# A two-layer attention on sorted edges: PSUM operands, rank one-hots per pass, lifted scores, a running maximum in two parts

## What is computed

```
h = (x @ W).reshape(n_nodes, H, C)
s_src, s_dst = einsum(h, a_src), einsum(h, a_dst)
e = s_src[src] + s_dst[dst]
e = where(e > 0, e, 0.2 * e)
e_max = segment_max(e, dst)
e_exp = exp(e - e_max[dst])
denom = segment_sum(e_exp, dst)
out = segment_sum(e_exp / denom[dst] * h[src], dst) + bias
```

## Time and profile before

| | us |
|---|---|
| median of 3 runs | 9747.82 |
| lowest and highest | 9736.4, 9757.34 |
| profiled execution: span | 9753.4 |

### The profile page before, as it was taken

One profiled execution on the slowest core, in us unless ns is written; L12 is line 12 of the kernel. 1 busy time (PEld: TensorE's weight loads), 2 busy tenths in 40 slices (PEclk: granted clock), 3 DMA queues, 4 the chain that ended last, 5 costly groups with the idle time before them and its releaser, 6 DMA issues. The chain is left out here.

```text
span 9753.4 us, 157815 instructions
## 1 busy us (share of the span) xinstructions
PE 6819.7 (70%) x40294; PEld 4632.6 (47%) x40295; DVE 4925.6 (51%) x14201; ACT 1511.9 (16%) x2248; POOL 3772.6 (39%) x3460
## 2 busy tenths in 40 slices
PE   0466304666666549999977777767777769996999
PEld 0345203344332225555546666656666635553555
DVE  6877805555554432222227788878888830113011
ACT  1222101111111111000002222222222200000000
POOL 1777875555542200000007677747777600000000
PEclk6688756776776669999988888878888879997999
DMA  0222101222221315686751111111111146653666
GB/s 15 54 70 70 35 9 59 76 78 71 71 71 59 55 49 163 173 197 173 179 139 46 45 44 45 44 44 45 45 44 45 41 121 190 190 170 104 190 192 183
DMA packets 871576, 901.10 MB, mean 92 GB/s; under 512 B 421539, under 2 KB 820226, under 8 KB 864867
## 3 DMA queue, kind: packets, MB, share of 16 engines
q1 hardware_dynamic: 753541, 637.16, 23.8%
q0 software_dynamic: 109664, 179.92, 8.3%
q10 hardware_dynamic: 8064, 80.29, 2.0%
HBM read 722.84 MB, written 93.87 MB: 84 GB/s over the span
## 5 line engine op out<-in xcount | busy, mean ns | idle before, releaser
L1900 POOL DMA_INDIRECT d_row_ring<-table_att,src_at x1664 | 1901.3, 1143 | 778.3 <-issue 495.0
L2411 PE MATMUL psum<-e_a_ring,e_parts 128*128 128x448 bf16 x8232 | 1578.6, 353 | 83.3 <-DVE e_parts L2493 76.1
L786 PE MATMUL psum<-b_hot 128*128 x2860 | 884.2, 452 | 1046.6 <-DVE b_hot L958 957.3
L769 POOL DMA_INDIRECT b_row_ring<-edge_attr,b_entry x896 | 880.0, 982 | 983.6 <-SPq L747 743.5
L2411 PEld LDWEIGHTS psum<-e_a_ring,e_parts 128*128 128x128 bf16 x8232 | 806.5, 98 | 824.6 <-issue 88.6
L786 PEld LDWEIGHTS psum<-b_hot 128*128 x2860 | 314.5, 110 | 1561.6 <-issue 1435.5
L352 POOL DMA_INDIRECT listed<-a_record,a_slot_no x832 | 932.9, 1121 | 318.5 <-issue 275.9
L1925 PE MATMUL psum<-edges_out,edges_in 128*128 128x112 f32 x4896 | 823.3, 338 | 168.0 <-ACT edges_in L1987 140.9
L1925 PEld LDWEIGHTS psum<-edges_out,edges_in 128*128 128x128 f32 x4896 | 768.4, 247 | 216.1 <-issue 190.4
L1311 PE MATMUL psum<-c_a_ring,c_parts 128*128 128x448 bf16 x4116 | 810.5, 355 | 45.2 <-DMA c_a_ring<-adjacency 40.6
L956 DVE TENSOR_SCALAR b_hot<-b_iota,b_key_id (+1 forms) x1430 | 387.3, 271 | 832.2 <-issue 640.9
(11 more groups left out here) (422 smaller groups left out, 7764.8 us busy)
## 6 DMA issues: line engine op xcount, KB each, us to landing
e_a_ring<-adjacency SPq DMA_DIRECT2D x1372, 224.0 KB, 2.8
c_a_ring<-adjacency SPq DMA_DIRECT2D x686, 224.0 KB, 2.9
adjacency<-b_line ACTq DMA_DIRECT2D x49, 1568.0 KB
a_cum<-edge_attr SPq DMA_DIRECT2D x103, 512.0 KB
d_row_ring<-table_att,src_at POOLq DMA_INDIRECT x1664
b_row_ring<-edge_attr,b_entry POOLq DMA_INDIRECT x896
listed<-a_record,a_slot_no POOLq DMA_INDIRECT x832
e_a_left<-adjacency_left SPq DMA_DIRECT2D x28, 224.0 KB, 3.1
```

Source lines behind the costliest of these rows:

```text
L769: pool.indirect_dma_start(out=row_ring[:, u % 4, g, 0:D], out_offset=None, in_=a["edge_attr_128"], in_offset=bass.IndirectOffsetOnAxis(ap= ...
L786: mm = nc.tensor.matmul(ps[:, v, :], hot[:, at, j, 0:P].rearrange("p a f -> p (a f)"), hot[:, at, j, P + v * WIN:P + (v + 1) * WIN].rearra ...
L1900: pool.indirect_dma_start(out=row_ring[:, u % 4, g, :], out_offset=None, in_=table_att[layer], in_offset=bass.IndirectOffsetOnAxis(ap=src_ ...
L2411: mm = nc.tensor.matmul(psum[:, 2 * (turn % 2) + v, 0:WIN], parts[:, piece, s, :], a_ring[:, s % SEVEN, v * WIN:(v + 1) * WIN], start=(s = ...
```

## The change

`RANKS` stays 6, and `WITH` = 28 cells per column become `SLOTS` = 24: the counting column is gone. `key_now` (now f32), `lifted` and `probs` lie in PSUM, and the three `ps_slots` banks move up by one. The one-hots of the ranks are made for all columns once in a pass, in bf16, and `enter` lifts the source scores of its batch by `lift` in their place. `lift` is the sum over the partitions of the largest absolute source score in each, made once in a layer with a matmul against ones. So every rank that is there has a score above zero and an empty cell has zero; `absent` and `shown` go, and the reduction reads PSUM itself. `to_lifted` takes the lift off again. The running maximum is cut to its upper 24 bits, so that two bf16 parts hold it exactly; the third stays zero (`to_edge` is cleared once). The clamp at zero goes. In the last stage the search's two semaphores become one.

```diff
-            WITH = SLOTS + HEADS
-            AGAIN = P // WITH
+            AGAIN = P // SLOTS
...
-            key_now = sbb("key_now", [P, TC], I16)
+            spare = psum[:, 1:3, :].rearrange("p a f -> p (a f)")
+            key_now = spare[:, 0:TC]
...
-            rank_hot = sbb("rank_hot", [P, G, RANKS])
-            absent = sbb("absent", [P, G, RANKS + 1])
-            shown = sbb("shown", [P, HEADS, G * (RANKS + 1)])
...
+            lifted = spare[:, TC:TC + G * HEADS].rearrange("p (g f) -> p g f", f=HEADS)
+            rank_hot = tables[:, 0:TC * RANKS // 2].bitcast(BF16).rearrange("p (c r) -> p c r", r=RANKS)
+            at = (G - 1 + AGAIN_SPREAD) * SPREAD
+            probs = psum[:, 6, at:at + G * HEADS].rearrange("p (g f) -> p g f", f=HEADS)
...
-            peak_rest = sbb("peak_rest", [P, HEADS])
+            peaks_cut = sbb("peaks_cut", [P, HEADS])
...
-            ps_slots = [psum[:, 2 + h, 0:G * WITH].rearrange("p (g s) -> p g s", g=G) for h in range(3)]
+            ps_slots = [psum[:, 3 + h, 0:G * SLOTS].rearrange("p (r f) -> p f r", f=HEADS) for h in range(3)]
...
+                nc.gpsimd.memset(to_edge[:], 0.0)
...
-                        mm = nc.tensor.matmul(psum[:, 2 + h, c * WITH:(c + AGAIN) * WITH], is_dst[:, h, c, :],
-                                              bc(ranked[:, h, c, :], 1, [P, AGAIN, WITH]), start=True, stop=True)
+                        mm = nc.tensor.matmul(psum[:, 3 + h, c * SLOTS:(c + AGAIN) * SLOTS], is_dst[:, h, c, :],
+                                              bc(ranked[:, h, c, :], 1, [P, AGAIN, SLOTS]), start=True, stop=True)
...
+                    pe.wait_ge(s_lift, 2 * layer + 1)
+                    nc.tensor.matmul(psum[:, 7, 0:1], ones[:], largest[:], start=True, stop=True).then_inc(s_lift, 1)
...
-                A, B, C, E_ = Stage(s_A, 1), Stage(s_B, 12), Stage(s_C, 4), Stage(s_E, 1)
+                A, B, C, E_ = Stage(s_A, 1), Stage(s_B, 9), Stage(s_C, 3), Stage(s_E, 1)
...
-                    A.by(V.tensor_tensor(rank_hot[:], bc(rank_now[:, mine], 2, [P, G, RANKS]),
-                                         bc(iota_k[:, 0:RANKS], 1, [P, G, RANKS]), ALU.is_equal))
                     if not first:
                         dve.wait_ge(s_out, at)
                     V.tensor_tensor(is_dst_b[:, h, :, :], bc(key_now[:, mine], 2, [P, G, P]),
                                     bc(iota_all[:, bass.ds(tile * P, P)], 1, [P, G, P]), ALU.is_equal).then_inc(s_hot, 1)
                     hold(dve, s_rows, units_at[0] + batch + 1, s_held_dve)
+                    A.by(V.tensor_scalar(lifted, rows_at(batch)[:, :, FEAT:], lift[:], None, ALU.add))
                     A.settle(dve)
-                    V.tensor_tensor(ranked[:, h, :, 0:SLOTS].rearrange("p g (r f) -> p g r f", f=HEADS),
-                                    bc(rank_hot[:], 3, [P, G, RANKS, HEADS]),
-                                    bc(rows_at(batch)[:, :, FEAT:], 2, [P, G, RANKS, HEADS]), ALU.mult).then_inc(s_rs, 1)
+                    V.tensor_tensor(ranked[:, h, :, :].rearrange("p g (r f) -> p g r f", f=HEADS),
+                                    bc(rank_hot[:, mine, :], 3, [P, G, RANKS, HEADS]),
+                                    bc(lifted, 2, [P, G, RANKS, HEADS]), ALU.mult).then_inc(s_rs, 1)
...
-                    mine = to_logit[:, one, :].rearrange("p a f -> p (a f)")
+                    mine = to_lifted[:, one, :].rearrange("p a f -> p (a f)")
...
+                    B.begin(at)
+                    B.by(V.tensor_copy(to_edge[:, h, 0, :, :], mine_parts))
                     dve.wait_ge(s_slots, at + 1)
-                    B.begin(at)
-                    B.by(V.tensor_tensor(absent[:], bc(iota_k[:], 1, [P, G, RANKS + 1]),
-                                         ps_slots[h][:, :, SLOTS:SLOTS + 1].broadcast_to([P, G, RANKS + 1]), ALU.is_ge))
-                    B.by(V.tensor_copy(to_edge[:, h, 0, :, :], mine_parts))
-                    B.settle(dve, 1)
-                    B.by(V.scalar_tensor_tensor(
-                        shown[:], bc(absent[:].rearrange("p g r -> p (g r)"), 1, [P, HEADS, G * (RANKS + 1)]), FAR,
-                        psum[:, 2 + h, 0:G * WITH].rearrange("p (r f) -> p f r", f=HEADS), ALU.mult, ALU.add))
-                    B.settle(dve)
-                    B.by(V.tensor_reduce(top[:], shown[:], AX_X, ALU.max))
+                    B.by(V.tensor_reduce(top[:], ps_slots[h], AX_X, ALU.max))
...
-                    B.by(V.tensor_copy(to_edge[:, h, 1, :, 0], peaks[:]))
-                    B.by(V.tensor_tensor(drop[:, h, :], now, peaks[:], ALU.subtract))
+                    B.by(V.tensor_scalar(peaks_cut[:].bitcast(I32), peaks[:].bitcast(I32), 8, 8, ALU.logical_shift_right,
+                                         ALU.logical_shift_left))
+                    B.settle(dve)
+                    B.by(V.tensor_copy(to_edge[:, h, 1, :, 0], peaks_cut[:]))
+                    B.by(V.tensor_tensor(drop[:, h, :], now, peaks_cut[:], ALU.subtract))
                     B.settle(dve)
                     dve.sem_inc(s_drop, 1)
-                    B.by(V.tensor_tensor(peak_rest[:], peaks[:], to_edge[:, h, 1, :, 0], ALU.subtract))
-                    B.by(V.tensor_copy(now, peaks[:]))
-                    B.settle(dve)
-                    B.by(V.tensor_copy(to_edge[:, h, 1, :, 1], peak_rest[:]))
-                    B.settle(dve)
-                    V.tensor_tensor(to_edge[:, h, 1, :, 2], peak_rest[:], to_edge[:, h, 1, :, 1], ALU.subtract).then_inc(s_me, 1)
+                    V.tensor_tensor(to_edge[:, h, 1, :, 1], peaks_cut[:], to_edge[:, h, 1, :, 0], ALU.subtract).then_inc(s_me, 1)
+                    B.by(V.tensor_copy(now, peaks_cut[:]))
...
-                    C.by(V.tensor_tensor(raw[:], raw[:], spread_sum[:, :, 1, :], ALU.subtract))
-                    C.settle(dve)
-                    V.tensor_scalar(shifted[:], raw[:], 0.0, None, ALU.min).then_inc(s_sh, 1)
+                    V.tensor_tensor(shifted[:], raw[:], spread_sum[:, :, 1, :], ALU.subtract).then_inc(s_sh, 1)
...
-                                    bc(probs[:], 3, [P, G, HEADS, W_HEAD]), ALU.mult).then_inc(s_W, 1)
+                                    bc(probs, 3, [P, G, HEADS, W_HEAD]), ALU.mult).then_inc(s_W, 1)
...
+                    st4.by(V.tensor_reduce(largest[:], every.rearrange("p t f -> p t f"), AX_XY, ALU.max, apply_absolute_value=True))
+                    st4.settle(dve)
+                    dve.sem_inc(s_lift, 1)
...
+                    dve.wait_ge(s_lift, 2 * layer + 2)
+                    st4.by(V.tensor_copy(lift[:], psum[:, 7, 0:1]))
+                    st4.by(V.tensor_scalar(to_lifted[:], to_logit[:], psum[:, 7, 0:1], None, ALU.subtract))
...
-                        ranks = Stage(s_pass, 3)
+                        ranks = Stage(s_pass, 4)
...
+                        ranks.by(V.tensor_tensor(rank_hot, bc(rank_now[:], 2, [P, TC, RANKS]),
+                                                 bc(iota_k[:], 1, [P, TC, RANKS]), ALU.is_equal))
...
-                        ranks.by(V.tensor_scalar(key_now[:], rank_now[:], float(RANKS), float(1 << 14), ALU.is_ge, ALU.mult))
+                        ranks.by(V.tensor_scalar(key_now, rank_now[:], float(RANKS), float(1 << 14), ALU.is_ge, ALU.mult))
...
-                        V.tensor_tensor(key_now[:], key_now[:], in_pass[:], ALU.add).then_inc(s_pass2, 1)
+                        V.tensor_tensor(key_now, key_now, in_pass[:], ALU.add).then_inc(s_pass2, 1)
...
-                        V.tensor_tensor(key_now[:], key_now[:], dst_at[:, 0:TC], ALU.add).then_inc(s_pass2, 1)
+                        V.tensor_tensor(key_now, key_now, dst_at[:, 0:TC], ALU.add).then_inc(s_pass2, 1)
...
+                            pe.wait_ge(s_count, 2 * i + 1)
+                            nc.tensor.matmul(psum[:, 7, 0:1], ones[:], hits[:], start=True, stop=True).then_inc(s_count, 1)
...
-                            dve.wait_ge(s_counted, i + (offset + 1))
+                            dve.wait_ge(s_count, 2 * i + (2 * offset + 2))
```

More of the change, by code:

```diff
@@ L12 @@
 AX_X = mybir.AxisListType.X
+AX_XY = mybir.AxisListType.XY
 RMAX = bass.bass_isa.ReduceOp.max
@@ L19 @@
 NONE = 9999
-FAR = -1e30
 class Count:
@@ L1738, in gnn_kernel @@
             b_att1 = sbb("b_att1", [P, D])
-            iota_k = sbb("iota_k", [P, RANKS + 1])
+            iota_k = sbb("iota_k", [P, RANKS])
             pass_base = sbb("pass_base", [P, P // RANKS + 2])
@@ L1753, in gnn_kernel @@
             weighted = flat_out[:, 0:G * FEAT].rearrange("p (g f) -> p g f", g=G)
-            ranked = flat_out[:, G * FEAT:G * (FEAT + 3 * WITH)].rearrange("p (u g f) -> p u g f", u=3, g=G)
+            ranked = flat_out[:, G * FEAT:G * (FEAT + 3 * SLOTS)].rearrange("p (u g f) -> p u g f", u=3, g=G)
             is_dst_b = flat_in[:, 3 * G * P * 3 // 2:6 * G * P].bitcast(BF16).rearrange("p (u g f) -> p u g f", u=3, g=G)
```

(26 more changed lines are left out.)

6 lines of the change are left out of this document (removed).

## The result

The changed kernel takes 9583.8 us (median of 4 runs, 9582.1 to 9587.7) against 9742.1 us (now the median of 4 runs of the kernel before): a ratio of 0.9834, with a 95% interval from 0.9823 to 0.9846. That is 158 us less, half of the 309 forecast, and 24 us above the top of the range. The profiled execution has a span of 9585.9 us, 167.5 less than before.

What follows compares the result with a forecast made beforehand. VectorE's own sequence was taken as the bound, GpSimd and TensorE close behind. A body falls 8.50 - 1.0 - 0.05 = 7.45 us: 319 us less, 10 more at layer starts, so 9748 - 309, rounded 9440 us; range 9375 to 9560.

Steps and rivals of the forecast that it cites:

- step (10): Start of each layer: one-hots of all columns read two SBUF tensors and may hold a gather, +5 us per layer.
- Steps (1) to (5): VectorE's body: `absent` and `shown` -0.53, reduction -0.03, peak before the mask -0.64, clamp -0.21, cut of the maximum +0.21 us.
- step (6): The lift on VectorE between mask and ranking, for which the ranking waits: +0.21 us a body.
- Step (7): Mask, ranking and weighting each read one operand from PSUM: no change in their time, 0.
- Step (8): GpSimd's gathers no longer wait for VectorE: a batch takes 9.9 us, staying behind VectorE's 11.0.
- rival A: GpSimd is the pace, its gathers not freed by PSUM operands: 98 us less per layer, about 9555 us; chance 8%.
- Step (9): TensorE follows: the mask clears the gather matmuls by 0.24 us; low-clock effects nearly cancel, 0.05 us a body gained.
- the term for fewer spells: Fewer spells of TensorE at its lower clock in the layers: 0.05 us less a body.
- Rival B: TensorE takes most back in normal clock through hand-overs or low spells: body 7.85 us, 9560 us; chance 8%.
- Rival C: Slower than before, TensorE left at 1.2 GHz: 10.7 us a body, 9930 us if half run so; chance 3%.

Runs made afterwards that it cites:

- e4: The kernel before with only the key (f32) and the probabilities in PSUM: 9739.2 us, ratio 0.9999.
- e9b: The kernel before with the wait for the gather matmuls moved from VectorE's mask to ScalarE's widening: 9695.7 us, ratio 0.9958.
- e1: The changed kernel with the wait for the gather matmuls moved from VectorE's mask to ScalarE's widening: 9463.5 us, ratio 0.9717.
- e2: The changed kernel with key and probabilities back in SBUF, the lifted scores staying in PSUM: 9578.4 us, ratio 0.9831.
- e6: e1 with eight more bf16 matmuls in each body of TensorE's loop, their results overwritten unread: 9460.4 us, ratio 0.9709.

## Why the prediction was wrong

**The reading of what bounds the kernel before held.** VectorE was the pace (e4: 521 us of idle GpSimd and no change in time), the gathers waited behind wide two-input instructions and are freed by a PSUM operand (951 ns), and the layer's start cost 4.5 and 3.6 us where 5 each was forecast, by the mechanism named in step (10): one gather of 6.10 us.

**Steps (1) to (5) held in sum, step (6) was too small.** With the wait moved in both kernels (e9b to e1) the body falls by 0.81 us, where 1.0 was summed and 0.05 more was taken for the clock. Ahead of the mask it falls by 0.97 of the 1.0. This 0.97 contains a cost that I had kept as a bound, the mask's run-time addresses: the idle time before the mask rises from 26.7 us (e9b) to 75.0 (e1), 0.16 us a body, and the other items saved that much more than summed. Behind the mask 0 was forecast (lift against clamp), and it became 0.15 longer: the lift costs 0.40 us where (6) had 0.21.

**Step (7) held**: PSUM as a source costs nothing here (1225 for 1226 ns, 1246 for 1254).

**Step (8) had the gathers right and their consequence wrong.** I wrote that without the freed gathers the gain would be that of rival A. e2 shows that with two of the three operands back in SBUF the changed kernel takes the same time: with bodies of 7.92 us a batch takes VectorE 11.7 us, and GpSimd's 8 x (1.07 + 0.30) = 11.0 still fits. The freed gathers were needed for my 7.45 us, not for what came.

**Step (9) is the one that failed, the overlap with TensorE.** "Moved by 1.0 it still clears by 0.24": the margin was measured from the end of the matmuls to the start of the mask with no hand-over in it. In the changed kernel the mask starts 0.46 us behind that end, and the row of before above had 0.30. 0.24 is less than either, so the mask waits even at the full clock (34.8 us of its wait). And "I let these nearly cancel", 0.05 us in favour, for the low clock: the clock rose, as said, from 0.87 to 0.92 and 0.93, but a spell that remains now meets a mask that is ready earlier: 95 masks wait 113.0 us with low clock in the body before them, where 46 waited 52.2. From weighting to mask 1.05 us less was forecast, and 0.73 less came.

**Where the missing 151 us are.** The forecast was 309 us less, 232 came where no mask waits for TensorE (e9b to e1), 158 with the wait. The wait of step (9) took 74 us. The other 77 are the 15 us of the term for fewer spells, 47 behind the mask (6), 10 ahead of it, and 5 that I can't place. The medians behind the 74 are each known to about 16 us, so the split is rough; the bodies of the traces give 0.81 - 0.58 = 0.23 us, 71 us, for the same. It is tempting to add up the wait's growth (96), the "issue" (30) and the missing term (15) to 141 of the 143 of the bodies. That sum is right by luck: it leaves out the 47 us behind the mask, and some 43 us by which the other items ahead of the mask saved more.

Rival B named the mechanism of step (9) and nearly the number (7.85 us a body against 7.92; 9560 against 9584), with a chance of 8%. The number is in part luck, as only half of the shortfall was the wait. It deserved much more than 8%, since the margin on which the forecast stood was a quarter of a microsecond, less than the hand-over of 0.30 us that the trace of before had.

Rival C, a low clock throughout, did not come; the mean granted clock rose.

## What to carry to other kernels

When an instruction stream gets shorter, list for each wait in it the time that the awaited work ends, with its hand-over, and take the saving of a stretch as the smaller of what is removed and what that end allows. Ask of each such wait what it protects: here the mask waited on behalf of the instruction after it on another engine, and putting the wait there was worth 120 us behind the change, beside the 158 of the whole change, and 45 us in the kernel before. To learn how much of a change a wait eats, move the wait in both kernels: after the change alone it looks larger than it is. A relief for an engine that is not the pace (PSUM operands for the sake of GpSimd's gathers) shows nothing until the next bound is lifted, so it is to be tried again then: 0 us in the changed kernel, 139 behind e1.

## What the runs showed of the hardware

A GpSimd gather that starts while VectorE runs a mask or a weighting with two SBUF inputs ends some 0.8 us after that instruction (0.82 in the median), and 0.81 us after the one-hots of 5.36 us. Of the gathers that start beside a mask, the median is 1.78 us before, with the key in SBUF, and 0.95 us with the key in PSUM, close to the 0.94 of a gather beside nothing. The Trainium skill's page "SBUF — State Buffer" (section "Who interferes with whom") says that two SBUF inputs contend with a GpSimd instruction that reads SBUF, and the trace agrees; the same section reports probes in which such an instruction did not stall a DMA, and here it holds the gather (6.10 us beside 5.36).

Adding 0.6 us of bf16 matmuls per body to TensorE made the kernel 61 us faster, with the granted clock at 0.99 instead of 0.94; where the mask did not wait for TensorE (e6 against e1) the same matmuls gave 3 us, within the noise. And chips differ: one took 23% longer for the kernel before (12005 us against 9741), with VectorE's and GpSimd's instructions of unchanged length and more time between them.
